# Attention inside a four-stage kernel: where the softmax sums are formed, how product matmuls are grouped, and where the steps of the division and of the maxima stand

## The chip, the cores and the metric

The kernel runs on one core of one Trainium2 chip. The metric is the device time of one execution in microseconds (us). Its engines are TensorE (PE; its weight loads are listed apart as PEld), VectorE (DVE), ScalarE (ACT), GpSimd (POOL) and SyncE (SP), which here only issues transfers (DMAs). Each engine runs its own list of instructions in order, and the lists are tied by semaphores.

## The reference

Four images of 128 channels and 1024 positions pass a non-local convolution, an attention layer with three branches, and a layer of experts. Only the attention is touched. Cut to what matters (16 heads, value width 32):

```python
q = jnp.concatenate([qn, qr], -1)
o1 = _attn(q, k1, v1, causal[None, None])            # branch 0: all earlier positions
o2 = _attn(q, ks, vs)                                # branch 1: 256 chosen positions
o3 = _attn(q, kw, vw, winmask[None, None])           # branch 2: a window of 64 positions
o = g[:, 0] * o1 + g[:, 1] * o2 + g[:, 2] * o3
return o.transpose(0, 2, 1, 3).reshape(B, T, N_HEAD * VDIM) @ Wproj

def _attn(q, k, v, mask=None):
    s = jnp.einsum('bhqd,bhkd->bhqk', q, k) / np.float32(np.sqrt(HD))
    if mask is not None:
        s = jnp.where(mask, s, jnp.float32(-1000000000.0))
    return jnp.einsum('bhqk,bhkd->bhqd', jax.nn.softmax(s, -1), v)
```

## The kernel before

The attention works on 32 *sides*: for each of the 4 images 8 pairs of heads (`HP` = 2). For each side there are two passes. The first finds the maximum of each row of scores, so that the second can take exponentials of scores less their maximum. The *preparation* of a side (function `preparation`) is a list of 42 *fills* and small steps: each fill lets PE write scores into one of 3 spare banks of PSUM (`SPARES`) and DVE reduce the bank to maxima (`max0` for branch 0, 24 of them; `max1` and `max2`, 8 each, for branches 1 and 2). `whole` joins partial maxima, and a `rows` step turns the maxima of a branch by a matmul, after which SP sends them as an extra row into the queries (`qb`, `q1b`). The *exact pass* (`exact_pass`) has 25 *units*. A unit is a block of 128 keys by up to 512 queries (a half `c` of the 1024) for both heads, with the keys on partitions: 9 units of branch 2 (64 to 192 queries wide, 1472 in sum), 4 of branch 1 (512 wide), 12 of branch 0 (128 to 512 wide); those of branches 0 and 1 are 6656 wide in sum. For each unit PE forms the scores of each head in one of 3 banks (`scores`), ACT writes their exponentials into `prob` (4 buffers, `PROBS`), and PE multiplies these in true float32 by the values and by a matrix of ones (`plain`): four matmuls of 32 output rows each, side by side in the four column groups of the array, two heads of values and two of ones. The ones give the softmax denominators. When the last unit of a branch and half is done, `sum` lets ACT copy values (scaled by the gate) to `products` and denominators to `sums`.

`window` mixes the exact pass of side w with the preparation of side w + 1, in shares that follow the columns of scores already passed. So all engines walk through 32 *windows*; window w starts with the scores of side w. Two sides make up one contraction of 128 rows. After each odd side the products of both are divided: `divide` steps, two pieces for each of 6 branch-halves, each a reciprocal on DVE and a multiplication on POOL (with an addition where branches are joined), then one projection `proj` per half on PE (float32, 4 records of 512), which DVE adds to the residual. Nearly all of these steps stand in the odd window; the last of them in the even window that follows.

One list `PLAN.steps` sets the order on every engine: PE, ACT, DVE and POOL each take from it the steps that are theirs. SP has its own list: `whole(side)` loads the operands of branch 0, `local(side + 1)` those of branches 1 and 2 with their exact parts (`qb`, `kwb`, `ksb`) and values (`vw`, `vs`), all in two buffers, and `row` sends the maxima.

Names in the profile: L1317, L1320/L1323, L1325 are the scores of the exact pass, L1344 the products, L1250 to L1272 the fills, L1280 `rows`, L1286/L1287 the projection, L1370 the exponentials, L1381/L1383 the two copies of `sum`, L1425 the reciprocals, L1434/L1439 the reductions to maxima, L1400/L1403 the multiplication and addition on POOL.

## Time and profile before

| what | value |
|---|---|
| median of 3 runs | 2780.64 us (2779.1 to 2782.71) |
| the profiled execution's own time | 2781.34 us |
| its span, first to last instruction | 2779.4 us |
| busy in the span: PE, DVE, ACT, POOL | 83%, 59%, 46%, 24% |
| attention, from the first exponential to the store of its last result | 699.7 to 2389.9 us |
| an odd window, an even window | 52.9 us, 52.7 us |

An engine's busy share is an average over stages; windows, forms and timelines say more about one of them. The ends of matmuls in the profile are modelled, so the distance between the starts of two matmuls tells more than the duration of one. A row of the timeline may stand for several instructions of one kind (x2).

### The profile page before, as it was taken

The numbers are of one execution on the slowest core, as the hardware profiler recorded it, in microseconds if no ns is written. First come the engines' busy times: TensorE is split into PE (matmuls) and PEld (weight loads), VectorE is DVE, ScalarE is ACT, GpSimd is POOL, SyncE is SP. The second block draws the span as 40 slices with busy tenths as digits, with TensorE's granted clock in tenths as the row PEclk, the third lists the DMA queues.
The fourth block names the chain that finished last, engine by engine and source line by source line (L and its number), as shares of the span: only waits on it lengthen the run. The fifth ranks groups of instructions, "written<-read, shape, count | busy, mean of one in ns | idle before, by whom it ended". The sixth has DMA issues, their size and how long they took to land. (4 is left out here: it accounts for less than half of the span.)

```text
span 2779.4 us, 45396 instructions
## 1 busy us (share of the span) xinstructions
PE 2320.6 (83%) x16656; PEld 1545.5 (56%) x16656; DVE 1628.3 (59%) x3043; ACT 1266.2 (46%) x2777; POOL 669.8 (24%) x687
## 2 busy tenths in 40 slices
PE   5585858663999999999999999999999999601995
PEld 3464545442666666666666666566566666401884
DVE  4758575734466466466566576566565564450766
ACT  2354545440455555555455455555555555310442
POOL 0265656573011011011011011011010010145332
PEclk9697978765999999999999999999999999655997
DMA  2255555479547646556655565664664660611113
GB/s 97 97 219 184 216 187 201 172 269 226 126 93 146 132 101 139 122 118 131 127 121 122 120 136 114 136 129 104 137 137 96 138 130 10 158 39 47 48 53 110
DMA packets 222841, 360.53 MB, mean 130 GB/s; under 512 B 68794, under 2 KB 124701, under 8 KB 222240
## 3 DMA queue, kind: packets, MB, share of 16 engines
q1 hardware_dynamic: 216288, 348.43, 50.1%
q0 software_dynamic: 4320, 8.43, 0.9%
q8 instruction: 137, 2.24, 0.4%
q10 hardware_dynamic: 2016, 0.77, 0.2%
q14 instruction: 80, 0.66, 0.1%
HBM read 229.58 MB, written 126.56 MB: 128 GB/s over the span
## 5 line engine op out<-in xcount | busy, mean ns | idle before, releaser
L1370 ACT ACTIVATE prob<-ps 128x512 f32<-128x512 f32 (+5 forms) x1600 | 637.8, 441 | 665.8 <-PE ps L1325 656.3
L1434 DVE TENSOR_REDUCE maxima<-ps 128x1 f32<-128x512 f32 (+3 forms) x768 | 387.5, 547 | 291.4 <-PE ps L1250 147.0
L1344 PE MATMUL ps<-prob,plain 128*32 128x512 f32 (+5 forms) x3200 | 512.0, 443 | 0.0
L1400 POOL TENSOR_TENSOR products<-products,sums 128x256 f32<-128x256 f32 x192 | 140.8, 733 | 1540.3 <-DVE sums L1425 1539.0
L1439 DVE TENSOR_REDUCE maxima<-ps 128x2 f32<-128x512 f32 (+1 forms) x512 | 293.7, 606 | 192.6 <-PE ps L1261 98.4
L1425 DVE RECIPROCAL sums<-sums 128x256 f32<-128x256 f32 x192 | 331.9, 1736 | 97.6 <-ACT sums L1383 97.6
L1317 PE MATMUL ps<-q1a_s,k1a_s 128*128 128x512 f32 (+3 forms) x768 | 303.0, 395 | 0.0
L1325 PE MATMUL ps<-q1b_s,k1b_s 128*128 128x512 f32 (+3 forms) x768 | 301.1, 393 | 0.0
L1344 PE MATMUL ps<-prob,v_s 128*32 128x512 f32 (+3 forms) x1536 | 284.3, 491 | 0.0
L1250 PE MATMUL ps<-k1a_s,q1a_s 128*128 128x512 f32 (+3 forms) x768 | 234.5, 374 | 0.5 <-DVE maxima L1439 0.2
L1381 ACT ACTIVATE products<-ps,gates_a 64x512 f32<-64x512 f32 x192 | 131.0, 682 | 196.4 <-PE ps L1344 196.3
L1317 PEld LDWEIGHTS ps<-q1a_s,k1a_s 128*128 128x128 f32 x768 | 147.1, 192 | 126.8 <-issue 119.0
L953 POOL TENSOR_TENSOR pairs<-pairs 128x512 fp32r<-128x512 f32 (+1 forms) x112 | 135.5, 1218 | 287.6 <-ACT pairs L921 287.5
L1317 PE MATMUL ps<-qa_s,kwa_s 128*128 128x192 f32 (+2 forms) x576 | 175.5, 305 | 19.3 <-ACT prob L1370 15.7
L1325 PE MATMUL ps<-qb_s,kwb_s 128*128 128x192 f32 (+2 forms) x576 | 183.9, 322 | 0.0
L1317 PEld LDWEIGHTS ps<-qa_s,kwa_s 128*128 128x128 f32 x576 | 109.7, 190 | 95.6 <-issue 63.8
L1250 PEld LDWEIGHTS ps<-k1a_s,q1a_s 128*128 128x128 f32 x768 | 144.9, 196 | 19.2 <-DVE maxima L1434 8.4
L1325 PEld LDWEIGHTS ps<-q1b_s,k1b_s 128*128 128x128 f32 x768 | 151.4, 197 | 5.5
L1270 PE MATMUL ps<-kwa_s,qa_s 128*128 128x192 f32 x512 | 122.8, 322 | 32.8 <-DMA wvp_g<-wvp_dram 32.8
L1344 PEld LDWEIGHTS ps<-prob,plain 128*32 128x32 f32 x3200 | 147.2, 109 | 0.0
L1323 PE MATMUL ps<-window_k,ident_bf 128*128 128x192 bf16 (+2 forms) x576 | 141.3, 245 | 0.0
L920 ACT CAST pairs<-ps 128x512 fp32r<-128x512 f32 (+1 forms) x112 | 62.4, 557 | 155.1 <-PE ps L893 106.4
(333 smaller groups left out, 4889.8 us busy)
## 6 DMA issues: line engine op xcount, KB each, us to landing
qh_dram<-pairs SPq DMA_DIRECT2D x96, 512.0 KB, 2.7
kwh_dram<-pairs SPq DMA_DIRECT2D x64, 512.0 KB, 2.7
qa_s<-qh_dram SPq DMA_DIRECT2D x128, 256.0 KB, 4.7
kwa_s<-kwh_dram SPq DMA_DIRECT2D x128, 256.0 KB, 7.7
q1a_s<-qh_dram SPq DMA_DIRECT2D x128, 256.0 KB, 4.8
qb_s<-qh_dram SPq DMA_DIRECT2D x64, 256.0 KB, 9.3
kwb_s<-kwh_dram SPq DMA_DIRECT2D x64, 256.0 KB, 10.3
k1a_s<-k1ah_dram SPq DMA_DIRECT2D x32, 512.0 KB, 6.9
```

The costliest lines, as they stand in the source:

```text
L953: pool.tensor_tensor(lo.bitcast(F32R), lo, hi.bitcast(F32), ALU.subtract)\
L1250: mm = pe.matmul(bank[:, 0:k1 - k0], m.q1a[:, k, h, i * P:(i + 1) * P], m.k1a[:, k, k0:k1], start=True, stop=True)
L1317: pe.matmul(bank, kx, qx[:, k, h, q0:q0 + w], start=True, stop=False, skip_group_check=True)
L1323: pe.matmul(bank, m.ident_bf[:], m.window_k[:, at:at + w], start=False, stop=False, skip_group_check=True)
L1325: pe.matmul(bank, ky, qy[:, k, h, q0:q0 + w], start=False, stop=True, skip_group_check=True)\
L1344: mm = pe.matmul(ps[at:at + VD, SCORES + k % 2, q0 - c * CH:q0 - c * CH + w], w_, m.prob[:, n % PROBS, h, 0:w], start=first, stop=True, sk ...
L1370: act.activation(m.prob[:, u % PROBS, h, 0:w], ps[:, turn % SCORES, 0:w], ACT.Exp, scale=SCALE).then_inc(s["exp_done"], 1)
L1381: act.activation(m.products[rows, br, cc], ps[0:NW, SCORES + k % 2, :], ACT.Copy, scale=m.gates[0:NW, side // NSIDE % 2, br:br + 1])
L1400: pool.tensor_tensor(o, o, m.sums[:, br, cc], ALU.mult).then_inc(s["divided"], 1)
L1425: dve.reciprocal(total, total).then_inc(s["inverse_done"], 1)
L1434: ins = dve.tensor_reduce(partial[:, h, i, part:part + 1], bank[:, 0:w], AX, ALU.max)
L1439: ins = dve.tensor_reduce(negs[1 if kind == "max1" else 2][:, at:at + 2], bank.rearrange("p (i n) -> p i n", i=2)[:, :, 0:w], AX, ALU.max, ...
```

## The change

It does the following.

1. The denominators of branches 0 and 1 are no longer formed by a matmul with ones for each unit. POOL adds the exponentials of a branch-half into `acc` (`SUMMING`: the first two units are added to each other, each further one to the sum; where the second unit is narrower a copy fills the rest): 12 additions and 1 copy in a window. When a branch is complete, one step `total` has PE multiply `acc` by the ones, four matmuls of 512 columns, into a spare bank, and `take` has ACT copy the two halves to `sums`. There are 2 `total` and 2 `take` steps in a window.
2. The product matmuls of two units stand in one run: a unit of branch 1 or of the first half of branch 0 takes the first two column groups, a unit of the second half of branch 0, which is as wide, the other two. The 9 units of branch 2 keep their ones, and are now first in the window. Their order and the other 16 units' is new, `prob` has 6 buffers, and a buffer is also held until POOL has added it.
3. Division steps, `rows` of branch 0, `total`, `take` and `proj` are pinned to units (`pinned`), half of the divisions in each window. Fills are spread by DVE's load (`dve_columns`) and stand behind the products of their unit.
4. `qb`, `kwb`, `ksb`, `vw` and `vs` have one buffer instead of two, and their loads (`window_exact`, `local_exact`) are issued in the window before their use, behind 9 and 16 of its 25 units. Other loads are split accordingly.

```diff
+SUMS = [(2, 0), (2, 1), (1, 0), (1, 1), (0, 0), (0, 1)]
...
+def groups():
+    found = units()
+    sets = [found[2, c][i:i + 2] for c in range(NC) for i in range(0, len(found[2, c]), 2)]
+    short = found[1, 0] + found[1, 1] + found[0, 0]
+    return sets + [list(x) for x in zip(short, found[0, 1])]
+UNITS = sum(groups(), [])
+TOGETHER = [tuple(UNITS.index(x) for x in group) for group in groups()]
 LAST = [max(u for u, x in enumerate(UNITS) if x[:2] == k) for k in SUMS]
...
+LOCAL, WINDOWED = LAST[3] + 1, LAST[1] + 1
+OCCUPANTS = [-2, 0, 1, 2, 3, 1]
...
+def summing():
+    found, released, former = [], {}, {}
+    for u, (br, c, j, q0, w) in enumerate(UNITS):
+        if br == 2:
+            continue
+        if (br, c) not in former:
+            former[br, c] = u
+            continue
+        released[u] = len(found) + 1
+        if former[br, c] is not None:
+            released[former[br, c]] = len(found) + 1
+        found.append((u, br, c, former[br, c], q0 - c * CH, w))
+        former[br, c] = None
+    return found, released
+SUMMING, RELEASED = summing()
...
+PROBS = 6
...
+def pinned(w):
+    def divisions(side, br, c):
+        return [("divide", side, SUMS.index((br, c)), piece) for piece in range(PIECES)]
+    slots = {}
+    def pin(at, steps):
+        for slot, step in zip(at, steps):
+            slots.setdefault(slot, []).append(step)
+    if w > 0:
+        pin((1,), [("rows", w, 0)])
+    if 0 < w:
+        if w % 2 == 0:
+            pin((0, 1), divisions(w - 1, 1, 1))
+        pin((2, 3), [("total", w - 1, 0), ("take", w - 1, 0)])
+        if w % 2 == 0:
+            pin((5, 6, 8, 9), divisions(w - 1, 0, 0) + divisions(w - 1, 0, 1))
+            pin((10, 13), [("proj", w - 1, c) for c in range(NC)])
+    if w < SIDES:
+        if w % 2 == 1:
+            pin((6, 8, 11, 13), divisions(w, 2, 0) + divisions(w, 2, 1))
+        pin((19, 20), [("total", w, 1), ("take", w, 1)])
+        if w % 2 == 1:
+            pin((22, 24), divisions(w, 1, 0))
+    return slots
 def exact_pass(w):
...
+    slots = []
+    pins = pinned(w)
     for u in range(len(UNITS) + 1):
+        todo = []
         if u < len(UNITS):
             todo.append(("scores", w, u))
...
+            todo += [("acc", w, op) for op, x in enumerate(SUMMING) if x[0] == u]
+        ready = [group for group, follower in zip(TOGETHER, TOGETHER[1:] + [(len(UNITS),)]) if follower[0] == u]
+        for group in ready:
+            todo.append(("products", w, group))
+            todo += [("sum", w, k) for k in sorted(LAST.index(x) for x in group if x in LAST)]
+        slots.append(todo + pins.get(u, []))
...
+def dve_columns(step):
+    if step[0] == "max0":
+        return min((step[4] + 1) * CH, (step[3] + 1) * P) - step[4] * CH + 120
+    return {"max1": 2 * KEEP, "max2": 2 * WN, "rows": P, "whole": 0, "proj": CH, "divide": 1600}.get(step[0], -120) + 120
 def window(w, prepare):
...
+    slots = exact_pass(w)
+    length = [UNITS[u][4] + 160 for u in range(len(UNITS))] + [0]
+    fixed = [sum(dve_columns(x) for x in todo) for todo in slots]
+    wanted = sum(dve_columns(x) for x in prepare)
+    share = (sum(fixed) + wanted) / sum(length)
+    todo, at, room = [], 0, 0
+    for u, slot in enumerate(slots):
+        todo += [x for x in slot if x[0] != "total"]
+        room += length[u] * share - fixed[u]
+        while at < len(prepare) and (room >= dve_columns(prepare[at]) / 2 or u == len(UNITS)):
+            room -= dve_columns(prepare[at])
+            todo.append(prepare[at])
+            at += 1
+        todo += [x for x in slot if x[0] == "total"]
+    return todo
...
+            window_keys(0)
             local(0)
             whole(0)
+            window_exact(0)
+            local_exact(0)
+            window_keys(1)
             local(1)
...
             for side in range(1, SIDES):
+                if side > 1:
+                    row(side - 1, 0)
+                units_done(side - 2, len(UNITS))
                 whole(side)
+                units_done(side - 1, WINDOWED)
+                window_exact(side)
+                if side + 1 < SIDES:
+                    window_keys(side + 1)
+                units_done(side - 1, LOCAL)
+                local_exact(side)
+                for br in (2, 1):
+                    row(side, br)
...
+            row(SIDES - 1, 0)
...
+                elif kind == "total":
+                    pe.wait_ge(s["acc_done"], len(SUMMING) * side + max(n for n, x in enumerate(SUMMING) if x[1] == a[0]) + 1)
+                    for c in range(NC):
+                        for h in range(HP):
+                            at = c * NW + h * VD
+                            mm = pe.matmul(bank[at:at + VD, :], m.plain[:], m.acc[:, a[0], c, h, :], start=True, stop=True,
+                                           skip_group_check=True)
...
+            def product(side, u, at, weights):
                 br, c, j, q0, w = UNITS[u]
...
+                n, k = side * len(UNITS) + u, SUMS.index((br, c))
+                first = UNITS.index(next(x for x in UNITS if x[:2] == (br, c))) == u
+                if first and side * len(SUMS) + OCCUPANTS[k] > 0:
+                    pe.wait_ge(s["banks_free"], side * len(SUMS) + OCCUPANTS[k])
+                for h in range(HP):
+                    mm = pe.matmul(ps[at + h * VD:at + (h + 1) * VD, bank_of(side, k), q0 - c * CH:q0 - c * CH + w],
+                                   weights[h], m.prob[:, n % PROBS, h, 0:w], start=first, stop=True,
+                                   skip_group_check=True)
+                return mm
+            def products(side, group):
+                pe.wait_ge(s["exp_done"], HP * (side * len(UNITS) + group[-1] + 1))
+                for place, u in enumerate(group):
+                    br, c, j = UNITS[u][:3]
+                    if br == 0:
+                        once("late%d" % (side % 2), 16 * LATE * turn_no(side))
+                        values = [m.v1[:, side % 2, j, :]] * HP
+                    else:
+                        once("exact", 16 * EXACT * (side + 1))
+                        values = [(m.vs if br == 1 else m.vw)[:, j, h * VD:(h + 1) * VD] for h in range(HP)]
+                    if br == 2:
+                        product(side, u, 0, values)
+                        mm = product(side, u, NW, [m.plain[:]] * HP)
+                    else:
+                        mm = product(side, u, NW * place, values)
+                    mm.then_inc(s["products_done"], 1)
...
+                        old_side, old = divmod(u - PROBS, len(UNITS))
+                        if old in RELEASED:
+                            act.wait_ge(s["acc_done"], len(SUMMING) * old_side + RELEASED[old])
...
+                if kind == "take":
+                    br = step[2]
+                    n, rows = plan.fill_no["total", side, br], slice(NW * (side % 2), NW * (side % 2) + NW)
+                    act.wait_ge(s["fill_ready"], n + 1)
+                    for c in range(NC):
+                        ins = act.copy(m.sums[rows, br, c * CH:(c + 1) * CH],
+                                       ps[c * NW:(c + 1) * NW, 8 - SPARES + n % SPARES, :])
+                    ins.then_inc(s["taken"], 1)
...
+                if step[0] == "acc":
+                    side, op = step[1:]
+                    u, br, c, former, at, w = SUMMING[op]
+                    n = side * len(UNITS)
+                    new = m.prob[:, (n + u) % PROBS, :, :]
+                    total = m.acc[:, br, c, :, at:at + w]
+                    pool.wait_ge(s["exp_done"], HP * (n + u + 1))
+                    if side > 0:
+                        pool.wait_ge(s["fill_ready"], plan.fill_no["total", side - 1, br] + 1)
+                    if former is None:
+                        pool.wait_ge(s["acc_done"], len(SUMMING) * side + op)
+                        ins = pool.tensor_tensor(total, total, new[:, :, 0:w], ALU.add)
+                    else:
+                        old = m.prob[:, (n + former) % PROBS, :, :]
+                        if UNITS[former][4] > UNITS[u][4]:
+                            alone = UNITS[former][4] - UNITS[u][4]
+                            pool.tensor_copy(m.acc[:, br, c, :, 0:alone], old[:, :, 0:alone])
+                            old = old[:, :, alone:]
+                        ins = pool.tensor_tensor(total, old[:, :, 0:w], new[:, :, 0:w], ALU.add)
+                    ins.then_inc(s["acc_done"], 1)
+                    continue
...
```

Three places show how the lists of the engines move (a row is an instruction: line, operation, written and read tiles, rows by columns; xN for N alike; in brackets the semaphores waited for).

PE at two units of 512 queries late in window 9, before; `v_s` are the values of branch 0, `plain` the ones.

```order
L1325 MATMUL ps<-q1b_s,k1b_s 128x512
L1250 MATMUL ps<-k1a_s,q1a_s 128x512 [waits emptied]
L1253 MATMUL ps<-causal_q,ident_bf 128x128
L1344 MATMUL ps<-prob,v_s 32x512 [waits exp_done]
L1344 MATMUL ps<-prob,v_s 32x512
L1344 MATMUL ps<-prob,plain 32x512 x2
L1344 MATMUL ps<-prob,v_s 32x512 [waits exp_done]
```

PE at the first two 512-wide units of an even window now; `vs_s` are the values of branch 1.

```order
L1436 MATMUL ps<-qa_s,ksa_s 128x512 [waits exp_done]
L1444 MATMUL ps<-qb_s,ksb_s 128x512
L1455 MATMUL ps<-prob,vs_s 32x512 [waits banks_free,exp_done]
L1455 MATMUL ps<-prob,vs_s 32x512
L1455 MATMUL ps<-prob,v_s 32x512 [waits banks_free]
L1455 MATMUL ps<-prob,v_s 32x512
L1384 MATMUL ps<-kwa_s,qa_s 128x192 [waits taken]
L1386 MATMUL ps<-window_q,ident_bf 128x192
```

Before, two units take eight matmuls here, four of them with the ones; now four, two for each unit, with a wait between the two units where a half begins.

PE at the seam of an odd and an even window, before (the last products, `rows`, then scores of branch 1 and fills of the next side).

```order
L1344 MATMUL ps<-prob,plain 32x128 x2
L1280 MATMUL ps<-ident,maxima 16x128 [waits max_done,emptied]
L1317 MATMUL ps<-qa_s,ksa_s 128x512 [waits exp_done,rows1]
L1325 MATMUL ps<-qb_s,ksb_s 128x512
L1317 MATMUL ps<-qa_s,ksa_s 128x512 [waits exp_done]
L1325 MATMUL ps<-qb_s,ksb_s 128x512
L1270 MATMUL ps<-kwa_s,qa_s 128x192 [waits near1,emptied]
L1272 MATMUL ps<-window_q,ident_bf 128x192
```

PE at the third unit of an even window now, with `total` of the side before (L1400) and the scores of the fourth and fifth unit.

```order
L1455 MATMUL ps<-prob,vw_s 32x192 x2
L1455 MATMUL ps<-prob,plain 32x192 x2
L1400 MATMUL ps<-acc,plain 32x512 [waits acc_done,emptied]
L1400 MATMUL ps<-acc,plain 32x512 x3
L1436 MATMUL ps<-qa_s,kwa_s 128x128 [waits exp_done]
L1442 MATMUL ps<-window_k,ident_bf 128x128
L1444 MATMUL ps<-qb_s,kwb_s 128x128
L1436 MATMUL ps<-qa_s,kwa_s 128x128 [waits exp_done]
```

Wide scores with fills between them gave way to narrow scores (L1436, L1442, L1444) without fills, and `total` waits for POOL.

POOL at the first divisions of the attention (windows 1 and 2), before.

```order
L1400 TENSOR_TENSOR products<-products,sums 128x256 [waits inverse_done] x3
L1403 TENSOR_TENSOR products<-products 128x256 [waits divided]
L1400 TENSOR_TENSOR products<-products,sums 128x256 [waits inverse_done]
L1403 TENSOR_TENSOR products<-products 128x256 [waits divided]
L1400 TENSOR_TENSOR products<-products,sums 128x256 [waits inverse_done] x3
```

POOL in the latter part of an odd window now.

```order
L1552 TENSOR_TENSOR acc<-acc,prob 128x1024 [waits acc_done,fill_ready,exp_done] x2
L1557 COPY acc<-prob 128x2x128 [waits fill_ready,exp_done]
L1559 TENSOR_TENSOR acc<-prob 128x2x384
L1552 TENSOR_TENSOR acc<-acc,prob 128x2x384 [waits acc_done,fill_ready,exp_done]
L1552 TENSOR_TENSOR acc<-acc,prob 128x2x256 [waits acc_done,fill_ready,exp_done] x2
L1569 TENSOR_TENSOR products<-products,sums 128x256 [waits inverse_done]
L1572 TENSOR_TENSOR products<-products 128x256 [waits divided]
L1552 TENSOR_TENSOR acc<-acc,prob 128x2x128 [waits acc_done,fill_ready,exp_done] x2
```

POOL's additions, which follow the exponentials, share its queue with the multiplications, which follow DVE's reciprocals: the last two additions of a side stand behind a multiplication.

## Rows read from the trace of the kernel before

**Rows 1.** The page: span; busy time, share and instructions of the engines.

```profile
span 2779.4 us, 45396 instructions
PE 2320.6 (83%) x16656; PEld 1545.5 (56%) x16656; DVE 1628.3 (59%) x3043; ACT 1266.2 (46%) x2777; POOL 669.8 (24%) x687
```

**Rows 2.** Windows 7, 8 and 31: length, busy PE, PEld, DVE, ACT, POOL.

```profile
1069.60:1122.50 52.90, 52.01 (x432) 32.78 (x430) 38.40 (x55) 27.48 (x63) 10.28 (x14) 1.00 0.57 122
1122.50:1175.20 52.70, 51.32 (x432) 32.59 (x430) 26.45 (x47) 27.59 (x63) 1.45 (x2) 1.00 0.59 123
2336.90:2389.90 53.00, 43.28 (x338) 23.06 (x336) 21.56 (x14) 26.92 (x63) 11.70 (x16) 0.94 0.02 6
```

**Rows 3.** Window 8, product matmuls (L1344) alone: length, busy PE, PEld.

```profile
1122.50:1175.20 52.70, 16.16 (x200) 5.04 (x200) 1.00 0.59 123
```

**Rows 4.** Timeline of PE: start, duration; two 512-wide units of products.

```profile
1214.14 0.62 PE L1344 MATMUL ps<-prob,v_s 128*32 128x512 f32 x2
1214.16 0.62 PE L1344 MATMUL ps<-prob,plain 128*32 128x512 f32 x2
...
1214.61 0.60 PE L1344 MATMUL ps<-prob,plain 128*32 128x512 f32 x2
1215.03 0.60 PE L1344 MATMUL ps<-prob,v_s 128*32 128x512 f32 x2
```

**Rows 5.** Timeline of the weight loads (PEld), the same place.

```profile
1214.60 0.12 PEld L1344 LDWEIGHTS ps<-prob,v_s 128*32 128x32 f32 x2 [0.30 <-issue]
```

**Rows 6.** Timeline of PE: both projections of one pair of windows.

```profile
1216.33 1.10 PE L1286 MATMUL ps<-products,wvp_g 128*128 128x512 f32 x2 [0.26 <-issue]
...
1234.89 1.10 PE L1286 MATMUL ps<-products,wvp_g 128*128 128x512 f32 x2 [0.91 <-DVE maxima L1439]
```

**Rows 7.** Timeline: both heads of a narrow unit; then ACT's copy and the scores behind it.

```profile
1125.08 0.33 PE L1317 MATMUL ps<-qa_s,kwa_s 128*128 128x192 f32 x1
...
1125.46 0.28 PE L1317 MATMUL ps<-qa_s,kwa_s 128*128 128x192 f32 x1
...
1142.35 0.58 ACT L1383 COPY sums<-ps 64x512 f32<-64x512 f32 x1
...
1143.34 0.36 PE L1317 MATMUL ps<-qa_s,kwa_s 128*128 128x192 f32 x1 [0.36 <-ACT prob L1370]
```

**Rows 8.** POOL's groups by form: busy us, mean ns, idle before.

```profile
L1400 POOL TENSOR_TENSOR products<-products,sums 128x256 f32<-128x256 f32 x192 | 140.8, 733 | 1540.3 <-DVE sums L1425 1539.0
...
L946 POOL TENSOR_TENSOR pairs<-rope,pairs 128x512 fp32r<-128x512 f32 x64 | 83.7, 1308 | 0.0
...
L930 POOL TENSOR_TENSOR scr<-arena,scr 128x1024 fp32r<-128x1024 f32 x4 | 9.3, 2337 | 0.0
```

**Rows 9.** ACT's groups by form, windows 7 and 8.

```profile
L1381 ACT ACTIVATE products<-ps,gates_a 64x512 f32<-64x512 f32 x12 | 8.2, 683 | 12.4 <-PE ps L1344 12.4
L1383 ACT COPY sums<-ps 64x512 f32<-64x512 f32 x13 | 7.6, 583 | 0.2
L1370 ACT ACTIVATE prob<-ps 128x192 f32<-128x192 f32 x24 | 6.9, 331 | 7.2 <-PE ps L1325 7.1
```

**Rows 10.** DVE's groups by form, windows 7 and 8.

```profile
L1425 DVE RECIPROCAL sums<-sums 128x256 f32<-128x256 f32 x12 | 20.8, 1737 | 4.9 <-ACT sums L1383 4.9
L1434 DVE TENSOR_REDUCE maxima<-ps 128x1 f32<-128x512 f32 x24 | 15.7, 682 | 11.3 <-PE ps L1250 9.4 <-PE ps L1253 1.9
...
L1439 DVE TENSOR_REDUCE maxima<-ps 128x2 f32<-128x384 f32 x16 | 8.1, 538 | 4.2 <-PE ps L1272 4.2
```

**Rows 11.** DMA issues of windows 7 and 8: size of one, us to landing.

```profile
qa_s<-qh_dram SPq DMA_DIRECT2D x8, 256.0 KB, 4.3
...
vs_s<-vsh_dram SPq DMA_DIRECT2D x2, 64.0 KB, 11.3
```

**Rows 12.** Timeline of SP: start, duration; four loads issued in window 7.

```profile
1100.43 1.84 SPq L1156 DMA_DIRECT2D ksa_s<-ksh_dram  x4
```

**Rows 13.** Timeline of PE: the first scores of window 0.

```profile
698.42 0.80 PE L1317 MATMUL ps<-qa_s,ksa_s 128*128 128x512 f32 x1 [8.79 <-DMA qb_s<-mrows]
```

196 lines of the change are left out of this document (87 added, 109 removed).

## The prediction

> **What bounds the kernel now.** I read the page first: PE is busy 83% of the span, DVE 59%, ACT 46% [rows 1]. These are averages over four stages, so I cut the attention into its windows. The cut shows 32 stretches that repeat: an odd window takes 52.9 us and an even one 52.7, 105.6 a pair. In both PE is busy over 97% at a granted clock of 1.00 (the 2.4 GHz level); DVE is busy 38.4 and 26.5 us, ACT 27.5, POOL 10.3 and 1.5 [rows 2]. The reader is to see that twelve us more or less of DVE's work change a window by 0.2 us: PE sets the pace. A busy PE need not be a PE at its peak, so I read starts in the timeline. Two 512-wide units of products run in steps of 0.42 to 0.46 us; in each step two matmuls of values and two with ones begin within 0.02 us of each other, and a float32 product needs two steps [rows 4]. So a unit of width w costs w x 1.68 ns (0.86 us at 512), whatever its four column groups hold. Where does PE stand idle? Before the projections, 0.26 and 0.91 us a pair [rows 6], and where ACT's two copies of a branch-half (0.68 + 0.58 us [rows 9]) hold up the exponentials behind them, and with them the next scores, 0.36 us of idle [rows 7]. The rest is work, or bubbles too small to name.
>
> **The work removed from PE.** Products keep PE busy 16.16 us in a window [rows 3]. The widths add to 8128, so 13.65 us is streaming; 2.5 us over 13 runs of products is 0.2 us for entering and leaving a run. Branches 0 and 1 are 6656 wide and are now paired at equal width: 3328 x 1.68 ns = 5.6 us less. The two `total` steps add 2 x 0.86 = 1.7 us, and 0.2 us each for their run, 0.4. Net **-3.5 us** a window.
>
> This needs the two units of a pair to run side by side although a semaphore increment stands between them. The trace shows that PE looks past one: the next unit's weights begin to load at 1214.60, before the last, incrementing matmuls of the unit ahead start at 1214.61 [rows 4, 5].
>
> The Trainium skill has a rule that speaks about this run, in "TensorE: Matmul & The Clock Gate", Part 3 (What overlaps and what doesn't): weight loads overlap matmuls in flight only when their row group differs. All of these use all rows, so by the rule each weight load would add its own time, and 152 loads a window instead of 200 would save another 48 x 0.11 = 5.3 us, some 165 us over the attention, and the time would be 2537. The trace disagrees: loads of 0.12 us start while a matmul of the run is in flight and the step stays 0.43 us [rows 4, 5]; I add nothing for it and give it less than 0.01.
>
> **Waits removed.** The projections now stand behind units without fills, with DVE and the banks free and the reciprocals begun 5 units earlier: -(0.26 + 0.91) / 2 = **-0.6 us** a window.
>
> **Waits added.** (a) In even windows the first nine units are narrow and have only one fill, `rows` and `total` beside them. ACT there has 18 exponentials of mostly 0.33 us (5.6 with the 128- and 64-wide ones), the two late `sum` copies of the side before (2 x 0.68), `take` (2 x 0.58) and two full sums (2 x 1.27) [rows 9]: 10.6 us. PE has about 9.8: 18 heads, 0.38 us one of 192 [rows 7] and less the narrower ones, 6.2 in all; 1472 x 1.68 ns of products, 2.5; 1.1 of `total`. Where the two are this near and tied by 3 banks, I take 1.9 us of waiting; in odd windows with fills 0.6. Such a stall, 0.4 to 0.6 us against the pace without it, stood twice in a window before [rows 7]. Net **+0.3**. (b) The last runs of products wait for the exponentials of the unit just scored, since their two units go together; before, the earlier units' products covered that. One exponential and its hand-over, some 0.5 us: **+0.5**. (c) Fills come in bursts of 3 to 4 on 3 banks behind wide units. DVE takes 0.54 to 0.68 us for a fill [rows 10], PE 0.25 to 0.4. A burst of four lasts 2.4 us on DVE against 2.0 to 2.2 us of the slot on PE; over the dense 10 units, less the slack of the slots with products: **+0.7**. Nothing if the banks absorb it; 1.5 if each burst waits. (d) POOL. No row has these additions in this stage; the nearest has 128x1024 at 2.34 us, 128x512 at 1.31, 128x256 at 0.73 [rows 8]. Six of 1024, two of 768 (1.8 by the line between), two of 512, two of 256 and a copy (0.4, between nothing and the 0.73 of the same elements) are 22 us; with divisions 25 to 28 us of a window of 50. From its first addition to the `total` of branch 0 in the next window POOL has 25 us to do, PE 31. The last two additions stand behind a multiplication that waits for `take` and a reciprocal of 1.74 us [rows 10]; by my sums POOL is done 0 to 1 us before PE asks. **+0.15**, at most 1.
>
> ACT's load is equal: six gated copies and six plain ones a side before and after. Division steps cost what they did, on DVE and POOL, with PE's work as cover; without it, 1.74 us each.
>
> **Loads.** SP spends 0.46 us on an issue [rows 12]. The exact parts are issued behind 16 units' products; 5 issues and 2 rows take 3.2 us, and landing took 4.3 us at the head of a burst and 11.3 at the end of one of 18 [rows 11]. They now stand at the head of theirs: some 8 us, against 12 to 14 us of PE's work left in the window. Cost nothing; with the 11.3 it would be 0 to 2 us a window.
>
> **The ends.** Window 0 began after 8.8 us of waiting for rows of maxima that queue behind loads [rows 13]. Ten fewer loads stand ahead (4.6 us of issues): **-4**, between -7 and 0. The last window (53.0 us to the store [rows 2]) has no fills, and POOL bounds it: 13 us to the first addition, 25 on POOL, `total` and `take` 2.0, four reciprocals 6.9, multiplication, projection and addition about 5.5 as before: 52.5. **0**, within 3.
>
> **The sum.** -3.5 - 0.6 + 0.3 + 0.5 + 0.7 + 0.15 = -2.4 a window; 31 windows -75; with the ends -79. From the profiled execution's own 2781.3 us that is 2702; the median shown lies 0.7 lower, so 2702 holds for it too. Bounds: with no new wait at all -4.1 x 31 - 7 = -134, 2647; with each wait doubled and the start unchanged, (-3.5 - 0.6 + 3.3) = -0.8 x 31 = -25, 2756.
>
> **Rivals.**
> *Almost free waits.* The banks absorb bursts and ACT keeps up: -3.1 to -4.1 a window, 2647 to 2680. For it: 38.4 us of DVE work cost nothing before [rows 2]. Against: fills are now denser and the narrow units bare. 0.20.
> *Waits eat more than half.* ACT in even windows, or single-buffered loads that land late: -0.8 to -1.6 a window, 2727 to 2756. The trace would show the first scores of a window idle for `exact`, or for exponentials. 0.17.
> *The pairs do not run side by side* (the other side). The two units write different banks, and a wait may stand between them; then values cost the old 5.6 + 5.6 us and `total` is extra: +5.6 - 3.5 - 0.6 + 1 = +2.5 a window, 2860. It decides from the point where the step of a pair is over 1.6 times 0.43 us. Against: rows 4 and 5. 0.05.
> *POOL becomes the bound.* If the 128x1024 additions take more here than in rows 8, with two strided inputs and DVE at work beside them, PE waits at `total` in every window. The slack is about 6 us in 25: from 2.9 us an addition the gain shrinks, from 3.2 it is gone, at 3.4 us (25 us become 35) a window costs 1.6 us more than before, 2830. Against: multiplications of 0.73 us in mean all ran beside reciprocals and reductions. 0.05.
> *The change does nothing*, the saved work turning wholly into waits: 2775 to 2786. 0.03.
> Forecast, 2680 to 2727: 0.50.
>
> **How the numbers follow.** Within 0.2% (5.6 us) two versions of this kernel can't be told apart. Faster: 0.50 + 0.20 + 0.17 = 0.87; same 0.03; slower 0.10. For 8 in 10 I take the forecast (0.50), the upper two thirds of the free case (0.14) and nearly all of the third (0.16): 2655 to 2752.
>
> **What would show it.** A pair of windows of 100.8 us (105.6); product groups of branches 0 and 1 starting in steps of 0.43 us with four value matmuls each; POOL additions of 128x1024 near 2.34 us, POOL busy 25 to 28 us a window; PE idle in even windows among the narrow units, ended by ACT; no idle before projections; `total` idle under 1 us; window 0 starting near 694.5. Wrong would make me: steps of 0.86 us in pairs, idle ended by POOL at `total`, or idle ended by a DMA at a window's start.

## The result, and the profile after

The changed kernel takes 2790.28 us (median of 20 runs, 2783.6 to 2796.28), the kernel before 2782.36 in as many runs: ratio 1.003, 95% interval 1.0024 to 1.0036. It is **slower by 0.3%**, where 2702 us was forecast. The profiled execution has a span of 2790.7 us.

The page of the changed kernel, span and engines (as [rows 1]):

```profile
span 2790.7 us, 43153 instructions
PE 2272.0 (81%) x15120; PEld 1500.8 (54%) x15120; DVE 1632.0 (58%) x3043; ACT 1255.0 (45%) x2777; POOL 1369.7 (49%) x1103
```

The busy time of engines in windows 7 and 8, the columns as in [rows 2], then the same windows with the product matmuls alone (as [rows 3]):

```profile
1067.80:1119.30 51.50, 48.12 (x375) 29.80 (x374) 33.80 (x51) 27.32 (x64) 25.81 (x19) 1.00 0.58 125
1119.30:1174.10 54.80, 51.87 (x389) 32.44 (x389) 31.51 (x52) 27.05 (x62) 29.93 (x24) 1.00 0.58 127
...
1067.80:1119.30 51.50, 10.78 (x136) 2.94 (x136) 1.00 0.58 125
1119.30:1174.10 54.80, 10.78 (x136) 2.94 (x136) 1.00 0.58 127
```

A pair of windows takes 106.3 us instead of 105.6, though the products' busy time went from 16.16 to 10.78 us in each, and the two `total` steps add only 2.1. PE is now idle for about 3 us in each, where it was idle for 1 [rows 2]. So the work went, and waits came. To size them I took all PE records of windows 5 to 28. What lies between one matmul's start and the next, beyond the streaming of its columns, is counted as lost, under the name of the later one. Streaming is taken as one column a clock at 2.4 GHz, and two clocks for each record of float32 products, `total`, `rows` and projections; four side by side count once. Masks are the bfloat16 matmuls that add the causal and window masks to scores and fills. Mean us a window (small items left out):

```
                    before   changed   fills_by_columns
streaming            40.2     36.3      36.3
lost, all            12.7     16.9      13.9
 before fills         1.7      4.3       2.5
 before scores        3.4      4.15      2.85
 before products      1.95     2.75      2.9
 before `total`        -       0.65      0.3
 before projections   0.85     0.1       0.1
 before masks         4.6      4.8       4.9
```

The largest item is the fills, and it has two parts. The waits of PE in the attention of the changed kernel (the later matmul, what ended its wait; us in total, times, the longest):

```profile
PE ps L1364 <- ACT sums L1529: 34.1, 30, 1.2
...
PE ps L1364 <- DVE maxima L1606: 10.7, 30, 0.4
PE ps L1400 <- DVE maxima L1606: 9.8, 30, 0.4
...
PE ps L1364 <- DVE maxima L1611: 4.7, 15, 0.3
PE ps L1375 <- DVE maxima L1611: 3.5, 15, 0.2
```

One wait a window for ACT's `take` (L1529) makes up 34.1 us, the waits for DVE's reductions 28.7. Of the 2.6 us a window that the table has more before fills, 1.4 stand before the fill that waits for `take`, 1.0 before those that wait for DVE; the latter also hold up `total`.

The waits for DVE first. The timeline of PE in window 7 (start, duration, in brackets the idle time before it), then DVE's at the same place:

```profile
1095.27 0.56 PE L1364 MATMUL ps<-k1a_s,q1a_s 128*128 128x512 f32 x2
...
1095.72 0.48 PE L1364 MATMUL ps<-k1a_s,q1a_s 128*128 128x512 f32 x1
1096.56 0.39 PE L1364 MATMUL ps<-k1a_s,q1a_s 128*128 128x256 f32 x1 [0.36 <-DVE maxima L1606]
...
1101.66 0.23 PE L1367 MATMUL ps<-causal_q,ident_bf 128*128 128x128 bf16 x1
1102.23 0.44 PE L1364 MATMUL ps<-k1a_s,q1a_s 128*128 128x384 f32 x1 [0.35 <-DVE maxima L1606]
```

```profile
1095.82 1.82 DVE L1606 TENSOR_REDUCE maxima<-ps 128x1 f32<-128x512 f32 x4 [1.72 <-PE ps L1364]
1098.27 1.75 DVE L1606 TENSOR_REDUCE maxima<-ps 128x1 f32<-128x512 f32 x3 [0.64 <-PE ps L1364]
1101.49 1.86 DVE L1606 TENSOR_REDUCE maxima<-ps 128x1 f32<-128x512 f32 x4 [1.47 <-PE ps L1367]
```

Four fills stand in a row behind a product run. Three go out at PE's pace, 0.2 us apart; the fourth waits until DVE has emptied the first bank, and everything behind it on PE waits too. And DVE had been idle for 1.72 and 1.47 us just before. DVE has the time for them: the fills only come all at once.

The second place is a fill that finds its bank still held by `total`. Timeline of PE, then of ACT, window 7:

```profile
1107.96 1.06 PE L1400 MATMUL ps<-acc,plain 128*32 128x512 f32 x8 [0.30 <-DVE maxima L1606]
...
1111.95 0.49 PE L1364 MATMUL ps<-k1a_s,q1a_s 128*128 128x512 f32 x1 [1.24 <-ACT sums L1529]
```

```profile
1109.82 0.89 ACT L1503 ACTIVATE prob<-ps 128x384 f32<-128x384 f32 x2 [3.54 <-PE ps L1444]
1110.73 1.17 ACT L1529 COPY sums<-ps 64x512 f32<-64x512 f32 x2
```

`total` is done at 1109.0, and ACT sits idle for 3.54 us ahead of 1109.82; but `take` (L1529) stands behind the next unit's two exponentials, so the bank is held until 1111.9.

### The profile page after: what moved, and what is told of

It reads as the page before. It is cut to its first block and busy times, and to the rows that moved or that the text cites. A ratio compares the mean times of both kernels' runs of the same rounds, so it can differ in the third digit from the quotient of the medians.

```text
span 2790.7 us, 43153 instructions
## 1 busy us (share of the span) xinstructions
PE 2272.0 (81%) x15120; PEld 1500.8 (54%) x15120; DVE 1632.0 (58%) x3043; ACT 1255.0 (45%) x2777; POOL 1369.7 (49%) x1103
## 5 line engine op out<-in xcount | busy, mean ns | idle before, releaser
L1552 POOL TENSOR_TENSOR acc<-acc,prob 128x1024 f32<-128x1024 f32 (+3 forms) x256 | 414.4, 1619 | 325.3 <-ACT prob L1503 224.8
L1559 POOL TENSOR_TENSOR acc<-prob 128x1024 f32<-128x1024 f32 (+1 forms) x128 | 286.6, 2239 | 199.9 <-ACT prob L1503 199.9
L1597 DVE RECIPROCAL sums<-sums 128x256 f32<-128x256 f32 x192 | 323.5, 1721 | 30.9 <-ACT sums L1529 21.5
L1364 PE MATMUL ps<-k1a_s,q1a_s 128*128 128x512 f32 (+3 forms) x768 | 265.0, 409 | 53.5 <-ACT sums L1529 34.1
L1444 PE MATMUL ps<-q1b_s,k1b_s 128*128 128x512 f32 (+3 forms) x768 | 300.2, 393 | 0.0
L1436 PE MATMUL ps<-q1a_s,k1a_s 128*128 128x512 f32 (+3 forms) x768 | 284.3, 370 | 0.0
L1455 PE MATMUL ps<-prob,v_s 128*32 128x512 f32 (+3 forms) x1536 | 230.1, 498 | 6.4 <-ACT prob L1503 6.1
L1364 PEld LDWEIGHTS ps<-k1a_s,q1a_s 128*128 128x128 f32 x768 | 142.1, 195 | 167.1 <-DVE maxima L1606 68.3
L1436 PE MATMUL ps<-qa_s,kwa_s 128*128 128x192 f32 (+2 forms) x576 | 175.7, 305 | 22.4 <-ACT prob L1503 22.4
L1436 PEld LDWEIGHTS ps<-q1a_s,k1a_s 128*128 128x128 f32 x768 | 146.8, 191 | 82.8 <-ACT prob L1503 45.1
L1444 PE MATMUL ps<-qb_s,kwb_s 128*128 128x192 f32 (+2 forms) x576 | 185.2, 326 | 0.0
L1444 PEld LDWEIGHTS ps<-q1b_s,k1b_s 128*128 128x128 f32 x768 | 151.3, 197 | 5.8
L1436 PEld LDWEIGHTS ps<-qa_s,kwa_s 128*128 128x128 f32 x576 | 111.8, 194 | 72.2 <-ACT prob L1503 37.3
L1442 PE MATMUL ps<-window_k,ident_bf 128*128 128x192 bf16 (+2 forms) x576 | 143.1, 248 | 0.0
L1384 PEld LDWEIGHTS ps<-kwa_s,qa_s 128*128 128x128 f32 x512 | 103.3, 202 | 64.0 <-DMA wvp_g<-wvp_dram 39.4
```

Source lines behind the costliest of these rows:

```text
L1364: mm = pe.matmul(bank[:, 0:k1 - k0], m.q1a[:, k, h, i * P:(i + 1) * P], m.k1a[:, k, k0:k1], start=True, stop=True)
L1384: pe.matmul(bank[:, i * KEEP:i * KEEP + WN], m.qa[:, k, h, t * P:(t + 1) * P], m.kwa[:, k, h, k0:k0 + WN], start=True, stop=True, skip_gro ...
L1436: pe.matmul(bank, kx, qx[:, h, q0:q0 + w], start=True, stop=False, skip_group_check=True)
L1442: pe.matmul(bank, m.ident_bf[:], m.window_k[:, at:at + w], start=False, stop=False, skip_group_check=True)
L1444: pe.matmul(bank, ky, qy[:, h, q0:q0 + w], start=False, stop=True, skip_group_check=True)\
L1455: mm = pe.matmul(ps[at + h * VD:at + (h + 1) * VD, bank_of(side, k), q0 - c * CH:q0 - c * CH + w], weights[h], m.prob[:, n % PROBS, h, 0:w ...
```

## The experiments

All times are medians; the kernel before had 2781 to 2783 us beside them. Theory A is that saved work is lost again at the fills, B that POOL paces the kernel, C that the bank held until `take` does.

**1. Where the fills stand.** Three edits of the changed kernel's `window`. `fills_by_columns`:

```diff
-    todo, at, room = [], 0, 0
+    todo, at, room, seen = [], 0, 0, 0
...
-        while at < len(prepare) and (room >= dve_columns(prepare[at]) / 2 or u == len(UNITS)):
-            room -= dve_columns(prepare[at])
-            todo.append(prepare[at])
-            at += 1
+        seen += UNITS[u][4] if u < len(UNITS) else 0
+        n = len(prepare) * seen // sum(x[4] for x in UNITS)
+        todo += prepare[at:n]
+        at = n
```

> The changed kernel, but the fills of the maxima are given to the units by score columns as before the change (still written behind the product runs). In the changed kernel TensorE's lost time in front of fills is 4.3 us a window (1.7 before the change). Theory A (saved product work is given back at the fills, above all because they are bunched): an even window no longer leaves its bare narrow units without a fill, bursts of three and four mostly go, and about 1 to 1.5 us a window comes back: 2745 to 2765 us. Rival B (POOL's additions pace the kernel, through the six probability buffers): where fills stand is not the limit, 2780 to 2795 us. Rival C (the single-buffered take of the totals alone makes the waits): under 0.4 us a window, 2778 to 2790 us.

Measured **2702.4 us** (ratio 0.971, 0.970 to 0.972): 88 us below the changed kernel, more than any theory had. By the table it loses 1.8 us a window less before fills, 1.3 less before scores and 0.4 less before `total`. The rows of four are nearly gone (part 4), but so are the waits for `take`: no wait of PE at L1364 ended by L1529 is left. So this run alone does not tell the two apart. Its windows 7 and 8:

```profile
1047.60:1095.60 48.00, 47.18 (x379) 30.17 (x377) 31.59 (x51) 27.18 (x62) 26.11 (x19) 1.00 0.63 134
1095.60:1148.10 52.50, 50.88 (x387) 31.67 (x386) 32.77 (x54) 27.13 (x64) 29.84 (x24) 1.00 0.60 133
```

`fills_ahead` moves the fills to directly behind the scores, `fills_as_before` has both edits:

```diff
-        todo += [x for x in slot if x[0] != "total"]
+        todo += [x for x in slot if x[0] in ("scores", "acc")]
...
+        todo += [x for x in slot if x[0] not in ("scores", "acc", "total", "take")]
+        todo += [x for x in slot if x[0] in ("total", "take")]
```

> The changed kernel, but each unit's fills are issued directly behind its scores, ahead of the product run, as before the change; the shares by VectorE's load stay, and `total` and `take` stay where they are. Theory A: fills then fill the time in which the product run waits for exponentials, and the product run fills the time in which VectorE empties the banks, so both waits shrink: about 1 us a window, 2750 to 2770 us. Rival B (POOL's pace): within 5 us of the changed kernel, 2783 to 2795. Rival C (take): within 5 us too.

> Both edits of the other two runs together: fills shared out by columns and issued directly behind the scores, everything else as in the changed kernel. Theory A: the lost time in front of fills comes back near the 1.7 us a window of before, less what the occupied bank of `total` costs: 2.0 to 2.6 us a window, 2715 to 2735 us, faster than both kernels. Rival B: 2780 to 2795. Rival C: 2770 to 2785.

Measured 2768.7 and 2710.9 us. With packed shares the old place helps (by 21 us), with even shares it costs 8: the shares matter more than the place.

**2. The same part alone, on the kernel before.** The rule by DVE's load and the place behind the products, nothing else of the change.

> The kernel before, with only one part of the change: its fills are shared out by VectorE's load (same weights) and written behind the product runs. No totals, no pairs, no additions by POOL. Theory A (the distribution of the fills loses time by itself, since bursts of three or four stand on three banks and narrow units stand without a fill): 1 to 2.5 us a window, 2815 to 2860 us. Rival D (it loses only together with the spare bank that `total` holds and with the narrow units in one row): within 0.5 us a window, 2775 to 2798 us.

Measured **2867.6 us** (1.030, 1.029 to 1.032), 85 us more than before, beyond the range of either theory. Windows 7 and 8 take 57.4 and 53.6 us. So the rule and the place lose time by themselves, without `total` and pairs. But it is largely another loss than in the changed kernel: in every window `rows` waits 1.09 us for the whole maximum (35.0 us in all), in odd windows a projection 1.05 us for a reduction. By the measure of the table the lost time before `rows` rose by 1.3 us a window, before fills by 0.9 only, about 27 of the 85 us. It also has 9 fills beyond the third in a pair of windows. That the 85 us are near the 88 shows nothing more.

**3. Which load the rule spreads.** In `divisions_uncounted` a single number changes:

```diff
-    return {..., "divide": 1600}.get(step[0], -120) + 120
+    return {..., "divide": -120}.get(step[0], -120) + 120
```

> The changed kernel with one weight changed: in the rule that shares out the fills a step of the division counts 0 columns of VectorE's load instead of 1,720. Then only the fills themselves, the rows and the projections are weighed, and the even windows' narrow units have fills again. If what loses the time is that fills are kept away from the units with divisions and pile up behind them, most of the 88 us between the changed kernel and fills_by_columns comes back: 2705 to 2730 us. If it is the rest of the rule (fixed 160 columns a unit, weights of the fills), it stays at 2770 to 2795 us.

Measured **2706.8 us**. One weight carries 84 of the 88 us. `no_reciprocals` keeps the rule and takes the load itself away:

```diff
-                    dve.reciprocal(total, total).then_inc(s["inverse_done"], 1)
+                    dve.tensor_scalar(total, total, 0.002, None, ALU.mult).then_inc(s["inverse_done"], 1)
```

> The changed kernel, fills as they are, with VectorE's reciprocals (1.74 us each, 12 for two windows) left out: a product with a constant stands in their place (the same 128x256 elements), so that the outputs are scaled by a constant instead of divided. If fills wait because VectorE is inside a reciprocal (its load is what matters), the lost time falls by 1 us a window or more: 2730 to 2760 us. If they wait because more fills stand in a row than there are banks, whatever VectorE does in between, about the same remains: 2770 to 2790 us.

Measured 2789.9 us, no change, though DVE has 8.5 and 6 us less to do. Its windows 7 and 8:

```profile
1064.40:1115.80 51.40, 48.06 (x375) 29.77 (x373) 25.29 (x51) 27.30 (x62) 25.95 (x19) 1.00 0.58 125
1115.80:1170.70 54.90, 51.93 (x390) 32.49 (x391) 25.51 (x52) 27.14 (x63) 30.06 (x24) 1.00 0.57 127
```

The rule makes room for a load that costs nothing here, and the room is made by packing fills elsewhere.

**4. How packed fills cost.** By the written order, windows 7 and 8 of the changed kernel have 10 rows of four or five users of the spare banks with no scores or products between them, 11 fills beyond the third; the kernel before has none, `fills_by_columns` 2, `divisions_uncounted` none. That `divisions_uncounted` is still 4 us slower than `fills_by_columns` shows that the count alone doesn't decide: in its trace 15 fills wait for `take` again, 18.2 us. `capped` allows no fourth and passes it on; `clumped` issues the even shares of two units at once:

```diff
 capped
-        while at < len(prepare) and (room >= dve_columns(prepare[at]) / 2 or u == len(UNITS)):
+        row = sum(x[0] in ("rows", "proj", "total") for x in slot)
+        while at < len(prepare) and (room >= dve_columns(prepare[at]) / 2 and row < 3 or u == len(UNITS)):
+            row += 1
 clumped, on fills_by_columns
-        n = len(prepare) * seen // sum(x[4] for x in UNITS)
+        n = len(prepare) * seen // sum(x[4] for x in UNITS) if u % 2 or u == len(UNITS) else at
```

> The changed kernel with its own shares by VectorE's load, but no unit gets a fill that would be the fourth on the three spare banks: it goes to the next unit instead. In the pair of windows 7 and 8 that removes the 10 runs of more than three bank users in a row (11 fills beyond the third); the even windows' narrow units stay nearly without fills, and the dense part becomes longer (up to 14 units in a row with three). If the runs beyond the banks are the whole cause, 2700 to 2725 us. If the uneven spread itself is (narrow units bare, wide units full), 2770 to 2795. In between, the two share it.

> As fills_by_columns (2702.4 us), but the shares of two neighbouring units are issued together behind the second of them. Averaged over two units the spread is the same; runs of more than three bank users in a row go from 2 to 12 in a pair of windows (27 fills beyond the third). If such runs cost what they seem to in the changed kernel (0.2 to 0.4 us for each fill beyond the third, VectorE's 0.68 us less TensorE's 0.25 to 0.4), 2780 to 2860 us. If VectorE's emptying behind the scores hides it, 2700 to 2730.

Measured **2730.9** and **2842.9 us**. Windows 9 and 10 of `capped` (in its window 7 the clock fell), then 7 and 8 of `clumped`:

```profile
1156.90:1206.00 49.10, 47.09 (x378) 29.72 (x376) 32.26 (x51) 27.20 (x63) 25.67 (x18) 1.00 0.63 131
1206.00:1258.90 52.90, 50.54 (x387) 31.97 (x387) 32.77 (x52) 27.13 (x62) 30.17 (x25) 1.00 0.57 122
```

```profile
1086.50:1139.20 52.70, 49.29 (x377) 30.74 (x377) 31.64 (x51) 26.86 (x63) 26.39 (x20) 1.00 0.58 122
1139.20:1195.70 56.50, 53.05 (x385) 32.43 (x385) 32.21 (x52) 26.85 (x62) 29.43 (x24) 1.00 0.56 123
```

Removing 11 such fills a pair brought 59 us, adding 25 cost 140: over 15.5 pairs that is 59 / 15.5 / 11 = 0.35 and 140 / 15.5 / 25 = 0.36 us each, from both sides. It is a mean: between `fills_ahead` (9 such fills) and `fills_as_before` (1) it is 58 / 15.5 / 8 = 0.47, and each of these edits moves fills in other ways too. In `capped` the lost time before fills fell from 4.3 to 3.0 us a window, before `total` from 0.65 to 0.25, before scores from 4.15 to 3.6, and no fill waits for DVE any more. The waits for `take` stay, 37.9 us in 30 waits. `fills_by_columns` has none, so the other 29 us can be theirs as well as the uneven spread's that `capped` keeps (narrow units bare, dense stretches longer). No run takes the two apart.

**5. The bank that `total` holds.** `take` directly behind `total`, ahead of the next exponentials:

```diff
-        pin((2, 3), [("total", w - 1, 0), ("take", w - 1, 0)])
+        pin((2, 2), [("total", w - 1, 0), ("take", w - 1, 0)])
-        pin((19, 20), [("total", w, 1), ("take", w, 1)])
+        pin((19, 19), [("total", w, 1), ("take", w, 1)])
...
-        todo += [x for x in slot if x[0] != "total"]
+        todo += [x for x in slot if x[0] not in ("total", "take")]
...
-        todo += [x for x in slot if x[0] == "total"]
+        todo += [x for x in slot if x[0] in ("total", "take")]
```

> The changed kernel, but ScalarE's `take` of the totals stands in the same slot as `total`, ahead of the next unit's exponentials instead of behind them. In the trace of the changed kernel the fill behind `total` of the second branch waits 1.51 and 1.21 us for it. Theory A (this is one part of the loss at the fills): the waits fall to the length of two copies less what runs meanwhile, 0.5 to 0.9 us a window back, part of it given away since the next exponentials come 1.2 us later: 2768 to 2782 us. Rival C (the occupied bank is the main loss): 2745 to 2765. Rival B (POOL's pace): 2785 to 2795, or slower by the exponentials that come later.

> The changed kernel with fills shared by columns (as in the run fills_by_columns, 2702.4 us) and `take` directly behind `total` (as in take_directly). In the trace of fills_by_columns the fills still wait 1.3 us in two windows for `take`. If the two losses are separate, 0.4 to 0.6 us a window come back: 2683 to 2692 us. If they are one loss (with fills spread evenly the occupied bank hardly matters and the copies only move ahead of exponentials): 2697 to 2708 us.

Measured 2750.1 us on the changed kernel (-40), but 2716.5 beside even shares, 14 us *slower* than `fills_by_columns`. Timeline of ACT in `take_directly`: the copies start with `total`, and the exponentials follow at once:

```profile
1101.44 1.17 ACT L1529 COPY sums<-ps 64x512 f32<-64x512 f32 x2 [2.81 <-PE ps L1400]
1102.64 0.87 ACT L1503 ACTIVATE prob<-ps 128x384 f32<-128x384 f32 x2
```

In `take_directly` the lost time before fills fell from 4.3 to 3.0 us a window, which accounts for the 40 us. With even shares nothing waited for `take` (the 1.3 us that the expectation reads there are waits of two weight loads, not idle time of PE), so there was nothing to win, and the 1.17 us of copies ahead of the exponentials is the dearer place: the lost time before scores rose from 2.85 to 3.15 us a window, before projections from 0.1 to 0.3. The held bank costs only where fills press on the banks; the losses are not separate.

**6. POOL.** `half_additions` adds the exponentials of the first head only (`new`, `old` and `total` cut to head 0; the other head's sums are left out, its half of `acc` filled with ones):

> The changed kernel with its fills as they are, but POOL adds up the exponentials of the first head only (half of each addition's columns; the second head's sums are left out and its half of the accumulator is filled once with ones). POOL's additions are 2.34 us for 128x1024 and become about 1.3. Rival B (the kernel is paced by POOL: exponentials wait for a probability buffer, `total` for the last addition): 2740 to 2765 us. Theory A (POOL's work is off the path that ends last, the time is lost at the fills): 2775 to 2790 us.

Measured 2785.4 us, 5 us less with POOL relieved of some 9 to 11 us a window. POOL does not pace the kernel. Its groups by form in the changed kernel, windows 7 and 8:

```profile
L1559 POOL TENSOR_TENSOR acc<-prob 128x1024 f32<-128x1024 f32 x6 | 14.3, 2378 | 8.5 <-ACT prob L1503 8.5
L1552 POOL TENSOR_TENSOR acc<-acc,prob 128x1024 f32<-128x1024 f32 x6 | 14.3, 2377 | 13.3 <-ACT prob L1503 12.0 <-PE ps L1364 1.2
...
L1552 POOL TENSOR_TENSOR acc<-acc,prob 128x512 f32<-128x512 f32 x4 | 5.1, 1275 | 3.4 <-ACT prob L1503 2.6 <-PE ps L1364 0.8
```

**7. The seam between windows.** PE waits there for exponentials that stand behind ACT's copies of the last two sums, and the last product run waits for the unit just scored. In the changed kernel the first wait is 0.68 us and stands in even windows alone, not in each as the expectation for `columns_take_seam` has it; with even shares it is 0.24 us in every window. Timeline of PE in `fills_by_columns`:

```profile
1093.77 0.43 PE L1455 MATMUL ps<-prob,v_s 128*32 128x128 f32 x8 [0.37 <-ACT prob L1503]
1096.02 0.36 PE L1436 MATMUL ps<-qa_s,kwa_s 128*128 128x192 f32 x1 [0.24 <-ACT prob L1503]
```

The edit, in `Plan`; the four lines on products are only in the kernels named so:

```diff
+        for w in range(SIDES - 1):
+            late = [("products", w, TOGETHER[-1])]
+            steps = [x for x in steps if x not in late]
+            at = steps.index(("scores", w + 1, 0)) + 1
+            steps[at:at] = late
+            late = [("sum", w, k) for k in (4, 5)]
+            steps = [x for x in steps if x not in late]
+            at = steps.index(("scores", w + 1, 1)) + 1
+            steps[at:at] = late
```

> As columns_take, and ScalarE copies the last two sums of a window behind the exponentials of the second unit of the next window instead of ahead of the first. In the trace of the changed kernel TensorE waits 0.68 us there each window for the exponentials that stand behind these two copies (1.39 us), and in three windows its clock falls to half for the next 4 us. Theory: 0.3 to 0.5 us a window: 9 to 16 us below columns_take. Rival (the copies only move into the row of narrow units, where ScalarE is as short of time): within 4 us of columns_take.

> Fills by columns (2702.4 us), `take` where the change has it, and the last two sums of a window copied behind the exponentials of the next window's second unit, which brought 15 us beside `take` moved (2716.5 to 2701.6). If the gain is that of the first narrow units' exponentials, it is there without the moved `take` as well: 2685 to 2692 us. If it only repaired what the moved `take` had cost, 2699 to 2706 us.

> As columns_seam, and the last product run of a window is issued behind the scores of the next window's first unit. In the trace of fills_by_columns this run waits 0.62 us in each window for the exponentials of the unit scored just before. If that wait is filled by the scores (0.9 us of TensorE), 0.3 to 0.6 us a window: 9 to 18 us below columns_seam. If the scores' own exponentials, which now stand behind, only move the wait by one unit, within 4 us of it.

> The changed kernel with the division weighed at 0 (2706.8 us) and the two edits at the window's seam (last sums behind the next window's second unit, last products behind its first scores), which took fills_by_columns from 2702.4 to 2677.8. If the seam edits add to any spread, 2679 to 2688 us. If they need the spread by columns, 2695 to 2708.

> The changed kernel with one edit: the last two sums of a window are copied behind the exponentials of the next window's second unit. In its trace TensorE waits 0.68 us at each seam, and in windows 2, 10 and 30 the granted clock falls to 0.50 right behind that wait and the window is 1.57 us longer. If the wait is what lets the clock fall, no even window is 56.5 us any more, and with the wait gone 15 to 20 us come back: 2770 to 2775 us, as beside fills_by_columns (2702.4 to 2685.1). If the clock falls for another reason, some even windows stay 1.5 us above the others.

Measured 2701.6 (15 us below `columns_take`), 2685.1, 2677.8, 2695.9 and 2773.5 us. The moved sums bring 15, 17 and 17 us (beside columns and `take`, columns alone, the changed kernel); the products 7 more, less than expected. In `seam` some 4.7 of the 17 us can be falls of the clock, which the changed kernel's profile has and this one's has not (last section). Beside the uncounted divisions the two together brought only 11.

**8. The price tried on a new kernel.** `columns_seam_products` has 2 fills beyond the third in a pair of windows; the same cap as in `capped` moves them on.

> As columns_seam_products (2677.8 us), with no fill placed as the fourth on the three banks. In a pair of windows 2 fills move on by a unit. The two earlier pairs of runs gave the same price for such a fill: the changed kernel against capped 59 us / 15.5 pairs / 11 fills = 0.35 us, clumped against fills_by_columns 140 us / 15.5 / 25 = 0.36. By this price 2 x 0.35 x 15.5 = 11 us: 2664 to 2670 us. If the fills moved only make the next units later, within 4 us of 2677.8.

Measured **2663.8 us** (0.957, 0.956 to 0.959), 14 us less where the price said 11 (0.45 us each). It beats both kernels: 118 us below the one before. Its windows 7 and 8:

```profile
1039.20:1086.40 47.20, 46.98 (x380) 30.15 (x378) 29.98 (x49) 27.15 (x62) 25.24 (x18) 1.00 0.63 136
1086.40:1137.40 51.00, 50.61 (x388) 31.76 (x386) 34.42 (x55) 27.12 (x62) 30.65 (x25) 1.00 0.63 137
```

## Why the prediction was wrong

**The step that failed is waits added, (c)**: "Fills come in bursts of 3 to 4 on 3 banks behind wide units", set at +0.7, at most 1.5. The mechanism was right, the size was not: forbidding a fourth fill in a row brought 59 us, 1.9 us a window. The step set DVE's 2.4 us for a burst of four against the slot's 2.0 to 2.2 us of PE, as though the banks let a burst spread over its slot. They don't: PE goes through its queue in order, so the scores behind a fourth fill wait until DVE has emptied the first bank, and idle time of DVE earlier in the slot (1.72 us above) is of no use. There are 11 fills beyond the third in a pair of windows, at 0.35 us each. The kernel before had no row of four, so its trace could not show this price; the new order does show the rows of four, and my bound of 1.5 was set by averages where it should have come from counting them.

**A term was missing:** the fill that waits for `take`. The bank of `total` was never counted as held, so its wait stood at nothing without a reason. Its idle time is 34.1 us in 30 waits; moving `take` is worth 40 us here, 1.3 a window. Of the 2.9 us a window by which the sum was off, the two make up about 1.2 and 1.3, if they add. That they do no run shows: the two edits were not tried together, and the uneven spread may have a share of its own, which had no term either.

The other steps:
- *Work removed*, -3.5: products 16.16 to 10.78 and 2.1 for `total`, -3.3 in busy time. Pairs run side by side: their groups of four start at 1094.28 and 1094.73, a step of 0.45 us. By the weight-load rule weighed in the prediction the time would be 2537; nothing here came near that, and the step is still that of [rows 4].
- *Projections*, -0.6: lost time 0.85 to 0.1, right.
- *(a)*, narrow units: idle among them ended by ACT is there in even windows, 0.68 us at the seam and 0.71 five units on, and none over 0.15 us in odd ones; over the whole run such idle time went from 16.1 to 23.2 us, +0.2 us a window. Of the right size. The whole of the lost time before scores rose by 0.8; 0.5 of it went with the rows of four, in `capped`.
- *(b)*, last products, +0.5: lost before products +0.8, part of it this wait of 0.37 us.
- *(d)*, POOL, +0.15: halving its additions brought 5 us, 0.16 a window. 128x1024 takes 2.38 us, POOL is busy 25.8 and 29.9, `total` idle 0.30: as forecast, but for the even window.
- *Loads*, nothing: the exact parts land in 3.6 to 6.5 us and end no wait.
- *The ends*: window 0 starts at 698.7, 1.0 us earlier and not 4, but is 4.5 us shorter; the last stage with window 31 is 1.4 us longer (443.9 to 442.5).

Over windows 1 to 30 the mean went from 52.8 to 53.3: +0.5 where -2.4 was forecast, and 2.4 + 0.5 = 2.9 us a window, 90 us. `fills_by_columns` lacks both, the packed fills but for 2 in a pair of windows and the waits for `take`, and takes 2702.4 us. Its lost time before fills is 0.75 us a window above that of the kernel before, near the 0.7 forecast; but it spreads the fills by another rule than the one predicted, so that it meets 2702 is partly luck. The rival nearest to the result, "the change does nothing", had a chance of 0.03 and no mechanism; "waits eat more than half" had the direction, but named ACT and the loads.

## What to carry to other kernels

Work moved off the bounding engine only pays if its queue stays evenly mixed: count, in the new order, how many users of N buffers stand in a row, and price each one beyond N by the consumer's time less the producer's as a first estimate (here 0.68 us for a reduction less 0.25 to 0.4 for a fill, against 0.35 to 0.47 measured). Spread producer work by the queue that bounds (here PE's columns), not by the load of an engine with a third of its time free. And when a buffer gets a new kind of user, find where its release stands in the other engine's queue; whether to move it up depends on what it would then delay.

## What the runs showed of the hardware that was not expected

In windows 2, 10 and 30 of the changed kernel TensorE's granted clock fell from 1.00 to 0.50 (2.4 to 1.2 GHz) right behind the 0.68 us wait at the seam, for 3.4 us. Window 8 and window 10 at the same place (one us each; the columns as above, the granted clock is the third number from the end):

```profile
1120.00:1121.00 1.00, 1.00 (x14) 0.88 (x16) 0.64 (x2) 0.61 (x3) 0.92 (x2) 1.00 0.00 0
1226.00:1227.00 1.00, 1.00 (x5) 0.95 (x5) 0.00 (x0) 0.42 (x3) 0.92 (x3) 0.50 0.00 0
1227.00:1228.00 1.00, 1.00 (x7) 0.92 (x6) 0.88 (x2) 0.47 (x2) 1.00 (x2) 0.50 0.00 0
```

Each fall makes its window 1.57 us longer (56.45 against 54.88), 4.7 us in all, of the 11.2 us by which the profiled execution is slower than that of the kernel before (2792.57 to 2781.34 us). Window 8 has the same wait of 0.68 us and no fall. Other runs have it in other windows, at the same place: `take_directly` in 2, 10 and 28, `half_additions` in 4, 10 and 30, `no_reciprocals` in 28, `fills_ahead` in 16 and 26, `clumped` in 23. In `capped` it stands in windows 7 and 17, right behind a wait of 1.35 us for `take`. In the profiles of `fills_by_columns` and `seam` no window between the first and the last has a fall; in `seam` a wait of 0.74 us stayed five units further on, as in the changed kernel (0.71), without one. So a short wait can end in a fall, but what decides it in which window stays open.
